# Attention in steps of four units: passes between the scores, products in pairs

## The reference

```python
q = (t @ W_tgt.T + b_tgt) * mask;  k, v = split((c @ W_src.T + b_src) * mask)
scores = where(mask == 0, -inf, q @ k.T / sqrt(64))      # per batch and head
update = softmax(scores) @ v
x = x + tanh(g_xattn) * (concat([t, update]) @ W_out.T + b_out)
```

## Time and profile before

| what | value |
|---|---|
| median of 3 runs | 1825.09 us |
| the profiled execution's own time | 1822.27 us |
| its span | 1820.5 us |
| PE busy over the span | 1657.0 us (91%) |
| DVE, ACT, POOL busy | 1157.5, 817.9, 715.3 us |
| L729 POOL additions into `acc` | 188 of 2386 ns and 32 of 2402 ns in the mean |
| L1019 DVE reductions of the first pass | 512 of 688 ns |
| L761 ACT exponentials | 256 of 1115 ns |

### The profile page before, as it was taken

One profiled execution on the slowest core, in us unless ns is written; L12 is line 12 of the kernel. 1 busy time (PEld: TensorE's weight loads), 2 busy tenths in 40 slices (PEclk: granted clock), 3 DMA queues, 4 the chain that ended last, 5 costly groups with the idle time before them and its releaser, 6 DMA issues. The chain is left out here.

```text
span 1820.5 us, 23948 instructions
## 1 busy us (share of the span) xinstructions
PE 1657.0 (91%) x8713; PEld 1017.9 (56%) x8754; DVE 1157.5 (64%) x2199; ACT 817.9 (45%) x866; POOL 715.3 (39%) x314
## 2 busy tenths in 40 slices
PE   6888899999998999999999999999998697886867
PEld 5766678888886644455444544454445454544434
DVE  6777645334334767756776687667637849489792
ACT  2111113222221244433554355525655778787776
POOL 1131000000000188865777477747854416052250
PEclk9999999999999999999999999999999899898989
DMA  6656455544435231112132133202233020020201
GB/s 238 240 190 228 167 204 189 193 156 167 156 120 179 94 140 59 59 71 100 65 105 94 47 113 110 82 2 106 91 130 139 24 92 1 24 93 1 93 0 47
DMA packets 107811, 200.81 MB, mean 110 GB/s; under 512 B 7616, under 2 KB 33216, under 8 KB 107712
## 3 DMA queue, kind: packets, MB, share of 16 engines
q1 hardware_dynamic: 107712, 199.49, 31.3%
HBM read 124.75 MB, written 74.71 MB: 110 GB/s over the span
## 5 line engine op out<-in xcount | busy, mean ns | idle before, releaser
L729 POOL TENSOR_TENSOR acc<-acc,pr 128x1024 f32<-128x1024 f32 x188 | 448.7, 2386 | 131.2 <-ACT pr L761 114.5
L761 ACT ACTIVATE pr<-ps,mcol 128x1024 f32<-128x1024 f32 x256 | 284.4, 1115 | 363.7 <-PE ps L1452 360.9
L1019 DVE CUSTOM_DVE_ANT_0 junk<-ps,mbias 128x512 bf16<-128x512 f32 x512 | 333.1, 688 | 129.2 <-PE ps L1427 125.1
L1464 PE MATMUL ps<-pr,vv 128*64 128x512 f32 x1024 | 273.8, 616 | 0.0
L736 POOL TENSOR_TENSOR h_first<-h_first,last_tap 128x1023 f32<-128x1023 f32 x44 | 103.7, 2359 | 253.4 <-DVE h_first L1341 223.7
L710 POOL MEMSET nmt<- 128x128 f32 x1 | 0.2, 206 | 364.5 <-DVE chl L1226 364.5
L1427 PE MATMUL ps<-kh,qh 64*128 64x512 f32 x512 | 123.0, 452 | 13.2 <-DVE nmv L1019 11.9
L1534 PE MATMUL ps<-xiT,w1q 128*128 128x512 bf16 x491 | 117.6, 380 | 12.5 <-ACT xiT L751 5.7
L729 POOL TENSOR_TENSOR acc<-pr 128x1024 f32<-128x1024 f32 x32 | 76.9, 2402 | 122.6 <-ACT pr L761 122.6
L1427 PEld LDWEIGHTS ps<-kh,qh 64*128 64x128 f32 x512 | 50.9, 184 | 131.0 <-issue 99.3
L1691 PE MATMUL ps<-w2q,hq 128*128 128x512 bf16 x492 | 117.8, 390 | 3.4 <-ACT hq L930 2.4
(11 more groups left out here) (171 smaller groups left out, 3155.5 us busy)
## 6 DMA issues: line engine op xcount, KB each, us to landing
craw<-in_ctxT SPq DMA_DIRECT2D x8, 2048.0 KB, 9.4
xa<-in_x SPq DMA_DIRECT2D x8, 1024.0 KB, 6.3
wraw<-in_w1T SPq DMA_DIRECT2D x16, 512.0 KB, 7.4
wraw<-in_w2T SPq DMA_DIRECT2D x16, 512.0 KB, 7.8
q_split<-kqh SPq DMA_DIRECT2D x32, 256.0 KB, 2.0
q_split<-kql SPq DMA_DIRECT2D x32, 256.0 KB, 2.3
base<-lna SPq DMA_DIRECT2D x8, 1024.0 KB, 9.0
k_split<-kqh SPq DMA_DIRECT2D x32, 256.0 KB, 2.1
```

Source lines behind the costliest of these rows:

```text
L729: nc.gpsimd.tensor_tensor(acc[:, blk % 2, :], first, pr[:, (8 * blk + j) % NP, :], ALU.add).then_inc(pool_acc, 1)
L761: act.activation(pr[:, u % NP, :], ps[:, 2 * (u % 2):2 * (u % 2) + 2, :].rearrange("p a t -> p (a t)"), ACT.Exp, bias=mcol[:, (u // 64) * ...
L1019: dve.tensor_tensor_reduce(out=(junk1 if n < LEAD and n % 2 else junk)[:, e, :], in0=ps[:, first_bank(n) + e, :], in1=mbias[:, b % 2, kk * ...
L1464: last = pe.matmul(ps[64 * e:64 * e + 64, 6 + blk % 2, :], vv[g % 2][:, j, 64 * e:64 * e + 64], pr[:, u % NP, e * CH:(e + 1) * CH], start= ...
```

## The change

All loops now go in long steps `q` of four units (67 of them). On TensorE a long step is: four scores 4q to 4q + 3, with three first passes among them; two products; the fourth first pass; two products. The first of the passes goes ahead of the first score, unless the step before ended with a turn, sums or a projection (`banks_busy`), in which case it goes behind it. Products lag by two units as before. Turns, sums and projections are at the ends of long steps (`TQ`, `ZQ`, `YQ`), projections two at a time, in banks 5 and 4. The last sums go to bank 5. On VectorE `inverse` and `lower` come behind the first pass's reductions of a long step, `normal` behind the second's; `lower` is two long steps behind the sums. The layer norm's pieces lie at other places, and some are taken two at a time. Sizes, durations and numbers of instructions are the same.

```diff
-        ZBLK = {4 * blk + 6: blk for blk in range(LAST)} | {4 * LAST + 4: LAST}
-        TURNS = {8 * g - 3: g for g in range(1, NG)}
-        YS = {32 * (b + 1) + i: [(b, i)] for b in range(B - 1) for i in range(NT)}
-        MACROS = 132
+        ZQ = {2 * blk + 3: blk for blk in range(LAST)} | {2 * LAST + 2: LAST}
+        TQ = {4 * g - 2: g for g in range(1, NG)}
+        YQ = {16 * (b + 1) + 1 + i // 2: [(b, i), (b, i + 1)] for b in range(B - 1) for i in range(0, NT, 2)}
+        QUADS = 67
...
         def y_bank(b, i):
-            return 4 if b == B - 1 and i % 2 else 5
+            return 4 + (i % 2 if b == B - 1 else 1 - i % 2)
...
             def store_x2(b):
-                sp.wait_ge(dve_free5, use5["y", b, NT - 1] + 1)
+                for i in (NT - 2, NT - 1):
+                    sp.wait_ge(*y_added(b, i))
...
-            for s in range(MACROS):
+            for s in range(2 * QUADS - 2):
...
-                    if a == 0 and s - 2 in ZBLK:
-                        upper(ZBLK[s - 2])
+                    if a == 0 and s % 2 and s // 2 - 1 in ZQ:
+                        upper(ZQ[s // 2 - 1])
...
-                if k == 21:
+                if k == 20:
                     done(f"am{NT - 1}")
...
+            for q in range(QUADS):
+                for a in range(4):
+                    n = 4 * q + LEAD + a
                     if n < UNITS:
                         dve_tops(dve, n)
...
+                    if a == 0 and q - 1 in ZQ:
+                        inverse(ZQ[q - 1])
+                    if a == 0 and q - 2 in ZQ:
+                        lower(ZQ[q - 2])
+                    if a == 1 and q - 1 in ZQ:
+                        normal(ZQ[q - 1])
+                    if a == 2 and 32 <= 2 * q < 128:
+                        layer_norm(q // 16 - 1, 2 * q % 32)
+                if q in TQ:
+                    dve_rows(dve, TQ[q])
+                if q in ZQ:
+                    sums(ZQ[q])
...
+            for q in range(QUADS):
+                n = 4 * q + LEAD
+                banks_busy = q == 0 or q - 1 in TQ or q - 1 in ZQ or q - 1 in YQ
+                if not banks_busy:
+                    first_pass(n)
+                for a in range(4):
+                    if 4 * q + a < UNITS:
+                        score(4 * q + a)
+                    if q == 0 and a == 0:
+                        pe.wait_ge(dve_b, NCH * B_DVE_N)
+                    if banks_busy and a == 0:
+                        first_pass(n)
+                    if a % 2:
+                        first_pass(n + (a + 1) // 2)
+                for a in range(4):
+                    if 0 <= 4 * q - 2 + a < UNITS:
+                        product(4 * q - 2 + a)
+                    if a == 1:
+                        first_pass(n + 3)
+                if q in TQ:
+                    pe_rows(pe, TQ[q])
+                if q in ZQ:
+                    sums(ZQ[q])
+                for b, i in YQ.get(q, ()):
+                    project(b, i)
```

More of the change, by code:

```diff
@@ L366, in flamingo_gated_block, with z_bank, z_turned, y_added @@
                 inv["row", 0] = 1
-        for s in range(MACROS):
[L368 to L380, removed]
+        for q in range(QUADS):
+            for n in range(4 * q + LEAD, min(4 * q + LEAD + 4, UNITS)):
+                use4["a", n], use5["b", n] = len(use4), len(use5)
+            if q - 1 in ZQ:
+                inv["r", ZQ[q - 1]] = len(inv) + 1
+                inv["t", ZQ[q - 1]] = len(inv) + 1
+            if q in TQ:
+                use4["t", TQ[q]] = len(use4)
+                inv["row", TQ[q]] = len(inv) + 1
+            if q in ZQ and ZQ[q] < LAST:
+                use4["z", ZQ[q]] = len(use4)
+            elif q in ZQ:
+                use5["z", LAST] = len(use5)
+            for b, i in YQ.get(q, ()):
+                if i % 2:
+                    use4["y", b, i] = len(use4)
+                else:
+                    use5["y", b, i] = len(use5)
+        for i in range(NT):
+            use5["y", B - 1, i] = len(use5)
+        def z_bank(blk):
+            return 4 if blk < LAST else 5
+        def z_turned(blk):
+            return (dve_free4, use4["z", blk] + 1) if blk < LAST else (dve_free5, use5["z", blk] + 1)
+        def y_added(b, i):
+            return (dve_free4, use4["y", b, i] + 1) if b < B - 1 and i % 2 else (dve_free5, use5["y", b, i] + 1)
         def first_bank(n):
@@ L396, in y_bank @@
         def y_bank(b, i):
[L397 removed]
+            return 4 + (i % 2 if b == B - 1 else 1 - i % 2)
         def heads(n):
             of_both = (0, dve_free4, use4["a", n]), (1, dve_free5, use5["b", n])
[L401 removed]
+            return of_both
         def added(u):
@@ L776, in layer_norm @@
                 an, dn = b * LC_ACT_N, b * LC_DVE_N
-                if k == 10:
+                if k == 13:
                     act.wait_ge(dve_lc, dn + LC_DVE[f"aggr{NT - 1}"])
                     act.activation(rs2[:, 0, :], mv2[:, :, 1], ACT.Sqrt, bias=eps).then_inc(act_lc, 1)
-                if 12 <= k < 12 + NT:
-                    i = k - 12
+                for i in range(2 * (k - 15), 2 * (k - 15) + 2) if 15 <= k < 19 else ():
                     act.wait_ge(dve_lc, dn + LC_DVE["nmr"])
@@ L784, in layer_norm @@
                                    scale=rs2[:, 1, i:i + 1]).then_inc(act_lc, 1)
+                if 21 <= k < 21 + NT:
+                    i = k - 21
+                    act.wait_ge(dve_lc, dn + LC_DVE["asc"])
+                    act.activation(lnx[:, i, :], lnx[:, i, :], ACT.Identity, bias=magic, scale=asc[:, i:i + 1]).then_inc(act_lc, 1)
                 if 22 <= k < 22 + NT:
                     i = k - 22
[L787 to L790, removed]
                     act.wait_ge(act_lc, an + LC_ACT[f"r{i}"])
@@ L1044, in sums @@
                 dve.wait_ge(pe_z, blk + 1)
-                dve.transpose(zt[:], ps[:, 4, :]).then_inc(dve_free4, 1)
+                dve.transpose(zt[:], ps[:, z_bank(blk), :]).then_inc(z_turned(blk)[0], 1)
             def inverse(blk):
-                dve.wait_ge(dve_free4, use4["z", blk] + 1)
+                dve.wait_ge(*z_turned(blk))
                 dve.reciprocal(zr[:], zt[:].rearrange("p (a r) -> p a r", r=32)[:, :, 0]).then_inc(dve_inv, 1)
@@ L1091, in layer_norm @@
                     dve.tensor_tensor(nmr[:], nmr[:], rs2[:, 1, :], ALU.mult).then_inc(dve_lc, 1)
-                if 13 <= k < 13 + NT:
-                    i = k - 13
+                for i in range(2 * (k - 16), 2 * (k - 16) + 2) if 16 <= k < 20 else ():
                     dve.wait_ge(act_lc, b * LC_ACT_N + LC_ACT[f"n{i}"])
                     dve.tensor_reduce(amax[:, i:i + 1], lnx[:, i, :], AX.X, ALU.max, apply_absolute_value=True).then_inc(dve_lc, 1)
-                if k == 21:
+                if k == 20:
                     done(f"am{NT - 1}")
@@ L1103, in layer_norm @@
                     dve.tensor_scalar(adq[:, b, :], amax[:], deq1, None, ALU.mult).then_inc(dve_lc, 1)
-            for s in range(MACROS - 1):
-                for a in range(2):
-                    n = 2 * s + LEAD + a
+            for q in range(QUADS):
+                for a in range(4):
+                    n = 4 * q + LEAD + a
                     if n < UNITS:
                         dve_tops(dve, n)
[L1110 to L1121, removed]
+                    if a == 0 and q - 1 in ZQ:
[10 more added lines that the diff above has]
+                    sums(ZQ[q])
+                if q == 61:
                     dve.wait_ge(pe_pv, 16 * (NG - 1))
                     dve_diagonal(dve, 0)
-                for b, i in YS.get(s, ()):
+                for b, i in YQ.get(q, ()):
                     finish(b, i)
-                if s >= 32 and s < 128:
-                    layer_norm(s // 32 - 1, s % 32)
+                if 32 <= 2 * q < 128:
+                    layer_norm(q // 16 - 1, 2 * q % 32 + 1)
             for i in range(NT // 2):
@@ L1467, in product @@
                 if u >= DIRECT:
-                    pe.wait_ge(dve_free4, use4["z", LAST])
+                    pe.wait_ge(dve_free5, use5["z", LAST])
                     for e in range(2):
-                        pe.matmul(ps[64 * e:64 * e + 64, 4, :], ones[:, 0:HD], pr[:, u % NP, e * CH:(e + 1) * CH], start=u == DIRECT, stop=False)
+                        pe.matmul(ps[64 * e:64 * e + 64, 5, :], ones[:, 0:HD], pr[:, u % NP, e * CH:(e + 1) * CH], start=u == DIRECT, stop=False)
             def sums(blk):
                 pe.wait_ge(pool_acc, 7 * blk + (7 if blk < LAST else 3))
-                pe.wait_ge(dve_free4, use4["z", blk])
+                if blk < LAST:
+                    pe.wait_ge(dve_free4, use4["z", blk])
                 for e in range(2):
-                    last = pe.matmul(ps[64 * e:64 * e + 64, 4, :], ones[:, 0:HD], acc[:, blk % 2, e * CH:(e + 1) * CH],
+                    last = pe.matmul(ps[64 * e:64 * e + 64, z_bank(blk), :], ones[:, 0:HD], acc[:, blk % 2, e * CH:(e + 1) * CH],
```

(24 more changed lines are left out.)

16 lines of the change are left out of this document (7 added, 9 removed).

## The result

The changed kernel takes 1840.42 us (median of 6 runs, 1834.82 to 1842.04), the one before 1825.28. The ratio of the means is 1.0078, 95% interval 1.0062 to 1.0095; by the medians it is +15 us, against +23 forecast. The profiled execution took 1841.7 us.

A forecast was written before the change was run, and what follows sets the result against it. TensorE was taken to set the pace, as long as VectorE delivers in time. The terms 5.7 - 1.7 + 28.8 - 2.4 - 10 + 0.7 + 2 gave +23 us on 1825.1, so 1848, range 1816 to 1864.

The forecast's parts named there:

- pass distance of 1.91: On TensorE, two first passes start at least 1.91 us apart, because all share banks 4 and 5 and await both reductions.
- late step behind a turn: An odd long step following a turn, its first score ahead of its first pass, was to last 11.24 us.
- 16 steps named: Odd long steps, 13 after turns and 3 after projections, where `ul` was to reach VectorE 0.26 us behind GpSimd's addition.
- forecast of 28.8: Loss claimed from `ul` waiting for GpSimd's addition: 1.8 us in each of 16 odd long steps, +28.8 us.
- The sum: All terms over the whole kernel added together: +23 us.
- The late even step: Even long step, first score before first pass: 9.63 us against 9.42 for four old units, 27 times, +5.7 us.
- The early step: Long step with its first pass before its first score: 9.29 us, scores waiting for exponentials, 13 times, -1.7 us.
- The layer norm: New places of the layer norm's pieces were to cut waits per batch from 7.4 to 4 us, -10 in all.
- the 41 us: Most that fewer TensorE round trips into products could save: 0.70 us in each of 59 long steps, if nothing waits.
- `ul` slipping ahead of GpSimd: Rival: in late odd steps `ul` goes before GpSimd's addition, the 28.8 us loss vanishes, 1819 us; chance 0.2.
- the whole saving: Rival: neither pass distance nor exponentials hold TensorE, `ul` stays hidden and all saved round trips count, 1772 us; chance 0.05.
- a late GpSimd: Rival: GpSimd's additions run late, so `ul` collides in the 10 to 13 early steps too, 1868 us; chance 0.14.

## Why the prediction was nearly right

*What held.* The pass distance of 1.91 from the earlier trace rows was the 1.90 in the trace, and the late step behind a turn came out at 11.14 (forecast 11.24). `ul` collides in exactly the 16 steps named, by 0.26 to 0.27 us (forecast 0.26, from the earlier trace rows), and nowhere else among steps with passes. The forecast of 28.8 counted these steps against the 9.42 of four old units: measured like that they are 16 x (11.14 - 9.42) = 27.5. The kernel with `ul` moved answers another question, what remains of such a step without the collision (9.4 to 9.9), and gives 23.7 in the attention stage, 26.5 by the medians. The pair of kernels with an extra instruction shows that the time of arrival is the cause.

*What was off in size.* The sum was 8 us too high. Three terms the trace sets right directly:
- The late even step was put at 9.63 and took 9.55: `inverse` holds the second reductions a little less than I had added up. 27 x -0.08 = -2.2.
- The early step was put at 9.29 and took 9.17 (9.07, and the 0.10 that the sums behind it take over). Score 3 did wait, 0.25, but score 4 only 0.11 (0.22 forecast). 13 x -0.12 = -1.6.
- A term was missing. Sums behind a pair of products cost 0.86 more than the pair alone (1.77 + 0.96 against 1.87), behind a single product 0.96 (0.96 + 1.01 against 1.01). 30 x -0.1 = -3.
- These make 16, where 15 was measured. The late odd steps are right in this way of counting: 11.14, and the 0.10 of the sums, against 11.24.

*The layer norm,* -10 by estimate, has the size that the version in the old order shows (-12.7 by the medians, -11.3 in the stage). But I had counted it as a gain of the long step, and it is not one: it is a part of the change that works by itself. That it fits inside the long steps too is in part luck. I had put the waits before down to small instructions, and about 5 of the 22 us followed `ul` (3 x 1.7). For the waits after I had left 12 us to the scale chain; in the trace they are about 9 (steps 10, 14, 26 and 42 are 0.7, 0.2, 3.2 and 4.8 over the others), and most of them follows the mask bias (2.08 and 2.09 of idle time ahead of pass 4 in steps 26 and 42), which the sum did not contain.

*Where the 41 us went.* The switches were saved in full: four long steps of a group save 4 x 0.70 = 2.8 us. The group of the version without collisions takes 39.91 all the same. Against 8.74, two late steps give back 0.81 each, the one behind a turn 0.94, and the early one 0.43, which is 3.0, less 0.2 for the sums. By medians the change is the sum of -12.7 (layer norm's places), +2.6 (long steps, projections in pairs) and +26.5 (`ul`), if one compares the versions in turn: 1824.0, 1811.3, 1813.9, 1840.4. By the attention stage of their traces it is -11.3, +3.0 and +23.7: 724.6, 713.3, 716.2, 739.9.

*The rivals.* `ul` slipping ahead of GpSimd, forecast at 1819, is what the moved version does on purpose (1814). Neither the whole saving nor a late GpSimd appeared. What stays open is what limits the long step once VectorE's reductions are halved: an exponential ahead of score 4 and GpSimd ahead of `ul` are both in the trace, and no run separates them.

## What to carry to other kernels

When an order is made denser, count for every shared buffer the least time between two uses, from the one place in the trace where it binds; here passes 1.91 us apart took back most of what fewer switches saved, and exponentials ahead of scores 3 and 4 the rest. An instruction that can be locked out by another engine has a place and a time of arrival, and 0.26 us decide over 1.7: move it to where the other engine waits, and look there whether its own engine has room. And when a change has several parts, run each alone. The best kernel here was the old order with a side product of the change.

## What the runs showed that I had not expected

- A stalled pair of matmuls costs less than its wait: the score behind pass 2 starts beside the pass's second matmul (714.67 against 714.76).
- VectorE's reduction with one SBUF input (1.22 us over 1024 columns, L1127 and L1129) ran its full speed while GpSimd was adding, where the subtraction with two SBUF inputs ended 0.55 behind GpSimd's instruction whenever it had started beside it. But one SBUF input is no safe sign: the mask bias has one, and took 2.87 where it takes 0.69 to 0.80 alone; small ones of 128x8 took up to 2.38.
- With half the columns a reduction takes 0.42 us instead of 0.69, and the old order, in which TensorE hardly waits for VectorE by the group lengths, still gained 11.5 us. The trace says where (above), but no run says why.
